# Attention stage of a fused kernel: output product from split parts, turns and products between the queries, key-value products in pairs

## What is computed

```python
B, L, D = x.shape
H, dh = (HEADS, HEAD_DIM)          # 16 heads of 16
q = relu(x @ Wq) / SCALE; k = relu(x @ Wk) / SCALE
v = x @ Wv;  u = silu(x @ Wu)      # each split into heads
kv = jnp.einsum('bhlk,bhlv->bhkv', k, v)
out = jnp.einsum('bhlk,bhkv->bhlv', q, kv)
out = srms_norm(out) * u           # by the root of the mean square of a head's 16 values
return out.transpose(0, 2, 1, 3).reshape(B, L, D) @ Wo
```

## Time and profile before

| what | value |
|---|---|
| median of 3 runs | 1888.03 us (1887.62 to 1890.15) |
| profiled execution, its own time | 1887.28 us |
| its span | 1885.6 us |
| PE busy | 1742.8 us (92%) |
| attention stage, first to last record | 1310.5 to 1486.6 us |
| loop bodies 1, 2, 3 | 41.32, 41.17, 41.17 us |
| last batch, up to the next stage's first matmul | 32.13 us |
| granted clock of the whole span | 0.974 of 2.4 GHz |

### The profile page before, as it was taken

One profiled execution on the slowest core, in us unless ns is written; L12 is line 12 of the kernel. 1 busy time (PEld: TensorE's weight loads), 2 busy tenths in 40 slices (PEclk: granted clock), 3 DMA queues, 4 the chain that ended last, 5 costly groups with the idle time before them and its releaser, 6 DMA issues. The chain is left out here.

```text
span 1885.6 us, 26501 instructions
## 1 busy us (share of the span) xinstructions
PE 1742.8 (92%) x9613; PEld 1381.1 (73%) x9613; DVE 1432.4 (76%) x2198; ACT 1079.3 (57%) x1866; POOL 1060.5 (56%) x633
## 2 busy tenths in 40 slices
PE   6888989899898989877899999999999899999999
PEld 2456666666556566655788888888888688888888
DVE  4899999999999999999777566666355755655665
ACT  6777787877777786787433433334444443334433
POOL 3889999999999999999722101112445411110111
PEclk9898999999999999988999999999999999999999
DMA  6223233233333233253000000000000000000000
GB/s 197 84 80 107 95 105 97 87 111 96 97 97 105 95 104 101 91 170 98 1 1 1 1 1 1 1 23 6 1 0 0 1 12 12 12 12 12 12 11 12
DMA packets 59109, 101.40 MB, mean 54 GB/s; under 512 B 11120, under 2 KB 11248, under 8 KB 58864
## 3 DMA queue, kind: packets, MB, share of 16 engines
q1 hardware_dynamic: 58992, 99.88, 16.6%
HBM read 95.14 MB, written 4.72 MB: 53 GB/s over the span
## 5 line engine op out<-in xcount | busy, mean ns | idle before, releaser
L383 POOL TENSOR_TENSOR m_U<-m_U,m_C 128x1024 f32<-128x1024 f32 x255 | 600.8, 2369 | 25.7 <-DVE m_U L890 15.5
L525 PEld LDWEIGHTS m_y<-ident,m_U 128*128 128x128 f32 x2048 | 252.6, 148 | 118.0 <-issue 70.9
L890 DVE TENSOR_TENSOR_SCAN m_U<-m_dA,m_carry,m_U 128x512 f32<-128x512 f32 x256 | 310.6, 1263 | 5.1 <-ACT m_dA L758 4.8
L525 PE MATMUL m_y<-ident,m_U 128*128 128x128 f32 x2048 | 284.8, 285 | 30.3 <-POOL m_U L383 30.2
L890 DVE TENSOR_TENSOR_SCAN m_U<-m_dA,m_U 128x512 f32<-128x512 f32 x256 | 295.9, 1203 | 11.5 <-ACT m_dA L758 8.2
L758 ACT ACTIVATE m_dA<-high,m_negA 128x512 f32<-128x512 f32 x256 | 172.3, 685 | 71.5 <-DVE m_U L890 71.1
L758 ACT ACTIVATE m_dA<-even,m_negA 128x512 f32<-128x512 f32 x256 | 170.7, 684 | 54.0 <-DVE m_U L890 53.0
L1123 POOL TENSOR_TENSOR SW<-g_Rt 128x1024 f32<-128x1024 f32 x16 | 31.6, 1996 | 252.6 <-ACT g_Rt L1308 252.6
L1123 POOL TENSOR_TENSOR SW<-f_Rt 128x1024 f32<-128x1024 f32 x16 | 31.6, 1995 | 205.2 <-ACT f_Rt L1308 205.2
L1303 ACT ACTIVATE g_sil<-g_psG 128x512 f32<-128x512 f32 x96 | 57.4, 598 | 140.2 <-PE g_psG L1181 139.6
L1303 ACT ACTIVATE f_sil<-f_psG 128x512 f32<-128x512 f32 x96 | 57.4, 598 | 134.9 <-PE f_psG L1181 134.2
(11 more groups left out here) (375 smaller groups left out, 4316.0 us busy)
## 6 DMA issues: line engine op xcount, KB each, us to landing
m_C<-bc_rows SPq DMA_DIRECT2D x256, 256.0 KB, 3.2
m_B<-bc_rows SPq DMA_DIRECT2D x60, 256.0 KB, 3.5
even<-in_ffn_w SPq DMA_DIRECT2D x16, 256.0 KB, 5.0
out<-res SPq DMA_DIRECT2D x8, 512.0 KB, 2.8
res<-in_x SPq DMA_DIRECT2D x1, 3072.0 KB, 13.0
res<-in_x SPq DMA_DIRECT2D x2, 512.0 KB, 4.3
turned<-in_Wkvqu SPq DMA_DIRECT2D x1, 1024.0 KB, 4.7
high<-in_in_w SPq DMA_DIRECT2D x1, 512.0 KB, 4.3
```

Source lines behind the costliest of these rows:

```text
L383: pool.tensor_tensor(u, u, C[:, M % C_RING, :].unsqueeze(1).to_broadcast([P, PE_E, CHUNK]), ALU.mult).then_inc(hc_ready, 1)
L525: last = nc.tensor.matmul(y[:, t, j * P:(j + 1) * P], U[:, M % U_RING, j, t * P:(t + 1) * P], ident[:, :], start=False, stop=n == N - 1, i ...
L890: nc.vector.tensor_tensor_scan(u, dA[:, s % A_RING, :], u, carry[:, e, n:n + 1] if q else 0.0, ALU.mult, ALU.add).then_inc(scan_done, 1)
```

## The change

The output product gets split operands: `wo` is split once into `wos`, and each turned pair of tiles into `ogs`, its high part by ScalarE's copy (`back`), its low part by a new VectorE step `low_og`. Turns no longer take a place in the ring's count (`JOBS` 16 to 12) but have semaphores of their own (`og_turned`, `og_high`, `og_low`). TensorE's order in a body changes, VectorE's `scale` of half 1 moves ahead of `keep_kv`, and key-value sums are taken two tiles at a time. The wait on `square_ready` goes.

```diff
+        wos = sb("wos", [P, 2, KD, D], FP32R)
...
-        ogT = sb("ogT", [P, TILES, D])
+        ogs = sb("ogs", [P, 2, TILES, D], FP32R)
...
-        KV, BACK, Q, JOBS = 0, (8, 14), 10, 16
+        WO_LANDED, WO_HIGH, WO_LOW = 16, 17, 18
+        KV, Q, JOBS = 0, 8, 12
...
@@ TensorE, keys_values @@
-                    if j > 0:
+                    if j % 2 == 0 and j > 0:
+                        heads_kv(n, first, j - 2)
                         heads_kv(n, first, j - 1)
+                heads_kv(n, first, SEQ_TILES - 2)
                 if behind is not None:
                     behind()
                 heads_kv(n, first, SEQ_TILES - 1)
...
-            def output(b, half, first):
+            def output(b, half):
                 for i in range(2):
-                    pe.wait_ge(ring_free, first + i + 1)
+                    pe.wait_ge(og_low, 2 * HALVES * b + 2 * half + i + 1)
                     pe.wait_ge(out_free, 2 * HALVES * b + 2 * half + i + 1)
                     for h in range(2):
-                        for g in range(KD):
-                            last = nc.tensor.matmul(acc[:, i, h * D:(h + 1) * D],
-                                                    ogT[:, 2 * i + h, g * P:(g + 1) * P], wo[:, g, :],
-                                                    start=g == 0, stop=g == KD - 1)
+                        last = split_mm(acc[:, i, h * D:(h + 1) * D],
+                                        [([x[:, 2 * i + h, g * P:(g + 1) * P] for x in og_parts],
+                                          [m[:, g, :] for m in wo_parts]) for g in range(KD)])
                     last.then_inc(out_full, 1)
...
@@ TensorE, the body @@
-                output_turn(b, 0, 1, start(b) + BACK[0])
+                output_turn(b, 0, 1)
+                first = start(b) + Q
+                pe.wait_ge(og_low, 2 * HALVES * b + 1)
+                query(first, 0)
                 pe.wait_ge(kvh_ready, b + 2)
-                output(b, 0, start(b) + BACK[0])
-                queries(start(b) + Q)
+                output(b, 0)
+                query(first, 1)
+                pe.wait_ge(ring_free, first + 1)
+                output_turn(b, 1, 0)
+                pe.wait_ge(ring_free, first + 2)
+                output_turn(b, 1, 1)
                 for i in range(2):
-                    output_turn(b, 1, i, start(b) + BACK[1])
-                output(b, 1, start(b) + BACK[1])
+                    pe.wait_ge(og_low, 2 * HALVES * b + 2 + i + 1)
+                    query(first, 2 + i)
+                output(b, 1)
...
@@ ScalarE @@
+            def back(b, half, i):
+                act.wait_ge(og_turned, 2 * HALVES * b + 2 * half + i + 1)
+                nc.scalar.activation(ogs[:, 0, 2 * i:2 * i + 2, :].rearrange("p h d -> p (h d)"), ring[:, i, :],
+                                     ACT.Copy).then_inc(og_high, 1)
...
@@ VectorE @@
+            def low_og(b, half, i):
+
+                dve.wait_ge(og_high, 2 * HALVES * b + 2 * half + i + 1)
+                high, low = (ogs[:, part, 2 * i:2 * i + 2, :].rearrange("p h d -> p (h d)") for part in range(2))
+                nc.vector.tensor_tensor(low, ring[:, i, :], high.bitcast(FP32), ALU.subtract).then_inc(og_low, 1)
...
                 scale(b, 0)
+                scale(b, 1)
+                low_og(b, 0, 0)
                 keep_kv(b + 1)
-                scale(b, 1)
+                low_og(b, 0, 1)
...
@@ VectorE, last_sequence @@
+                for i in range(2):
+                    low_og(b, 0, i)
                 late = slice(TILES, SEQ_TILES)
...
                 add_output(b, 0)
+                for i in range(2):
+                    low_og(b, 1, i)
                 add_output(b, 1, True)
...
```

More of the change, by code:

```diff
@@ L1633, in _ @@
         def _(pe):
+            og_parts = [ogs[:, part, :, :] for part in range(2)]
+            wo_parts = [wos[:, part, :, :] for part in range(2)]
             def split_mm(out, terms):
@@ L1703, in heads_out, with output_turn @@
                     last.then_inc(ou_full, 1)
-            def output_turn(b, half, i, first):
-                pe.wait_ge(ring_free, first + i - 1)
+            def output_turn(b, half, i):
                 for h in range(2):
@@ L1743, in _ @@
             keys_values(0, KV)
-            queries(FIRST_Q)
-            pe.wait_ge(w_o, 16)
+            for i in range(KD * HALVES):
+                pe.wait_ge(ring_free, FIRST_Q + i - 1)
+                query(FIRST_Q, i)
+            pe.wait_ge(w_o, WO_LOW)
             with pe.Fori(0, BATCH - 1) as b:
@@ L1788, in keys_values, with query @@
                     nc.scalar.activation(kv[:, j, D:], ring[:, j % 2, D:], ACT.Copy).then_inc(ring_free, 1)
-            def queries(first):
-                for half in range(HALVES):
-                    for g in range(KD):
-                        i = KD * half + g
-                        act.wait_ge(ring_full, first + i + 1)
-                        nc.scalar.activation(qT[:, g, half * CHUNK:(half + 1) * CHUNK], ring[:, i % 2, :], ACT.Relu,
-                                             scale=Q_SCALE).then_inc(ring_free, 1)
+            def query(first, i):
+                half, g = divmod(i, KD)
+                act.wait_ge(ring_full, first + i + 1)
+                nc.scalar.activation(qT[:, g, half * CHUNK:(half + 1) * CHUNK], ring[:, g, :], ACT.Relu,
+                                     scale=Q_SCALE).then_inc(ring_free, 1)
             def heads_out(b, half):
@@ L1816, in _ @@
                 keys_values(start(b) + KV)
-                back(start(b) + BACK[0])
-                queries(start(b) + Q)
-                back(start(b) + BACK[1])
+                for half in range(HALVES):
+                    for i in range(2):
+                        back(b, half, i)
+                    for i in range(2):
+                        query(start(b) + Q, KD * half + i)
             for half in range(HALVES):
@@ L1835, in _ @@
                                      ACT.Copy)
-            back(start(BATCH - 1) + 2)
+            for i in range(2):
+                back(BATCH - 1, 1, i)
         @block.vector
@@ L1974, in _ @@
             nc.vector.tensor_scalar(norms.var[:, EARLY], norms.mv[:, EARLY, 1], EPS, None, ALU.add).then_inc(var_ready, 1)
+            for i in range(2):
+                low_og(BATCH - 2, 1, i)
             add_output(BATCH - 2, 1)
```

52 lines of the change are left out of this document (25 added, 27 removed).

## The result

The changed kernel takes 1901.41 us (median of 6 runs, 1900.58 to 1903.77) against 1888.42 us for the kernel before (6 runs, 1887.62 to 1890.15) in the same comparison. The ratio is 1.007, with a 95% interval of 1.0057 to 1.0083: slower, by more than the 0.2% that can be told from none. The profiled execution took 1901.13 us with a span of 1899.4, 13.85 more than the one before.

What follows compares the result with a forecast made beforehand. TensorE's order of work was taken as the bound in the attention bodies. Terms -5.2 + 8.5 + 4.0 + 2.5 = +9.8 us, with clock falls of +4.5 and +0.5 making +14.8, gave 1902.8 us; range 1896.5 to 1909.0.

Steps and rivals of the forecast that it cites:

- the case given as likeliest: Attention stage: both stalls come, with falls of TensorE's clock as reckoned; 1902.8 us, chance 0.55.
- First stall: After a body's first turns, TensorE waits for low_og behind VectorE's late scale of half 1; +8.5 us over three bodies.
- Second stall: After a body's second turns, TensorE waits for low_og behind add_output and statistics; +1.3 us per body, +4.0 in sum.
- the third body's link: Second stall in the third body: VectorE has one link more there, adding 0.1 us.
- Last batch: Before the last product, the second pair of low_og stands behind add_output with its statistics; +2.5 us.
- Split product: Output product on TensorE: 24 split matmuls replace 16 fp32 ones, saving 0.65 us per half over 8 halves; -5.2 us.
- Pairs: Key-value products taken in pairs free no waiting TensorE work; 0, with bounds of -0.5 and +0.5 us.
- Prologue: Splitting wo once, 0.6 us on ScalarE and 0.7 on VectorE, is hidden while TensorE runs queries; 0.
- The clock: TensorE's clock falls at the first stall, 1.5 us per body, +4.5; +0.5 for the last batch's longer pause.
- Rival (a): Attention stage: the stalls come but TensorE's clock stays up; +9.8 us, 1897.8 us, chance 0.22.
- Rival (c): Second half's factors are no brake, no first stall or clock fall; +1.3 us, 1881 without other waits; chance 0.05.
- (d): No difference: stalls and savings cancel within 0.2%, 3.8 us; chance 0.06.

Runs made afterwards that it cites:

- e5: Kernel before with only VectorE's scale of half 1 moved ahead of keep_kv, output product still fp32; 1898.92 us, ratio 1.0057.
- e1: Changed kernel with VectorE's scale of half 1 put back behind keep_kv and both low_og of half 0; 1891.53 us, ratio 1.0017.
- e10: Changed kernel with GpSimd's power for half 1 of each body taken over 8 of 16 heads; 1892.06 us, ratio 1.0022.
- e4: Changed kernel with twelve unread 512-column matmuls on TensorE in each body's first stall; 1898.99 us, ratio 1.0059.
- e2: Changed kernel with low_og of half 1 ahead of the tokens' statistics, in bodies and last batch; 1900.17 us, ratio 1.0066.
- e11: e7 with the output product in plain fp32 and no low_og; 1886.49 us, ratio 0.9995.
- e7: Changed kernel with body turns in ou's banks, two queries ahead of each product, VectorE's scale and statistics behind low_og; 1881.45 us, ratio 0.9963.
- e6: Kernel before with the key-value sums in pairs alone; 1888.16 us, ratio 1.0000.
- e8: Split output product and paired key-value sums, with TensorE's order of the kernel before; 1886.78 us, ratio 0.9993.
- e9: Changed kernel with six unread 512-column matmuls in each body's first stall; 1899.36 us, ratio 1.0061.
- e3: Changed kernel with the edits of e1 and e2 together; 1885.29 us, ratio 0.9987.

## Why the prediction was right

1902.8 us was predicted, 1901.41 measured, and the case given as likeliest is the one that came. The rise was over-forecast a little more than the total shows: +14.8 was predicted; the medians rose by 13.0 and the profiled executions by 13.85. The kernel before came out 0.4 higher in this comparison than in the one that the prediction had. Step by step:

- **Where the stall comes from.** "Nobody on TensorE's path needs the second half's factors yet" was the fact, and the new order made someone need them. Shown from three sides: e5 makes the stall with that exchange alone, e1 takes it away by undoing it, e10 takes it away by shortening the power.
- **First stall, +8.5.** The distance from second turn to next work grew by 2.64, 2.85 and 2.55: +8.0. e4 against e1 gives 7.8.
- **Second stall, +4.0.** First turn to next query grew by 1.2, 1.2 and 1.0: +3.4. The extra 0.1 for the third body's link did not show. The statistics are the wait that ends last, as predicted, but e2 shows that with them out of the way only 0.55 of the 1.2 us goes.
- **Last batch, +2.5.** 3.60 for 1.29: +2.3.
- **Split product, -5.2.** 24 records last 3.04 us, the last of them 0.28, so they follow each other by 2.76 / 23 = 0.120, where the 49 records of the next stage gave 0.1167. 24 take 2.88, and 0.57 per half is saved: -4.6. The term was mis-sized in the change's favour, by 0.6 us, and e11 against e7 has the same 0.57. The four passes of true fp32 of which the Trainium skill tells ("FP8 and Floating Point Precision", TensorE Precision Notes) would have made it 0.86 by the prediction's estimate: the trace does not agree.
- **Pairs, 0.** e6: 0.1 us.
- **Prologue, 0.** From the stage's first matmul to body 1 it takes 20.96 us, before 20.97.
- **The clock, +4.5 and +0.5.** The size was right, the places were not. The prediction had three falls in the bodies at 1.5 each; two came, at 1.56 and 1.26 by e4, and none in the third body, though it was idle for 2.87 us. That the third did not come is luck of the execution as far as the runs show: e2, with the same pause, had it. So the body that stayed at 43.6 us lies outside the 44 to 46 that the prediction named. In the last batch a fall was added that had a price of its own: 2.46 - 2.3 + 1.14 = 1.3 us is what remains for it, 1.5 by e2, where 0.5 was put. Together 1.56 + 1.26 + 1.3 = 4.1 against 5.0. The Trainium skill ("TensorE: Matmul & The Clock Gate", HAM oscillation) has the throttle come back with every long pause of a loop: bodies 1 and 2 of the trace agree, body 3 does not.

At full clock the measured parts are 8.0 + 3.4 + 2.3 - 4.6 = +9.1 where +9.8 was predicted. With 4.1 for the clock and 0.26 for the later start it makes 13.5 of the 13.85; of the rest, 0.4, some 0.24 stands in body 1 and was not followed.

Rival (a), stalls without falls in the bodies, is what e4 made: 1897.8 was given, 1898.99 measured. Rival (c) is e10: +1.3 us was given for it, and e1 and e10 lie 3.6 and 4.5 above the kernel before, in the main because the last batch keeps its added fall and the split saves less. Its two figures also do not agree: `scaled` over by 1400 is 2.24 us before 1402.24, and the power was to be 2.9 shorter. The 1881 us that (c) gave for all waits gone is what e7 reached, 1881.45. (d) did not come in the changed kernel.

## What to carry to other kernels

Before moving work ahead of a wait, look for the latest input of the step that is moved past, even if nobody waits for it yet: here a factor that came 28 us into each body, at no cost, stopped TensorE as soon as its reader stood one place earlier on VectorE. Compare the saving with the length of the path that the new operand adds (turn, copy, subtraction), and put independent matmuls there first: the same split product was worth nothing in the bodies of e8 and 1.14 us in each of e7. And count a stall of TensorE at its length and the clock's fall that may come with it, here 1.3 to 1.6 us each, behind idle stretches of 1.75 to 3.3 us, though not behind all of them. One profiled execution does not tell whether a fall belongs to a kernel.

## What the runs showed that was not expected

- The length of the last idle stretch does not decide whether the clock falls. The first stall of body 3 left TensorE idle for 2.87 us in the changed kernel, without a fall, and for 2.88 in e2, with one; 1.75 us brought a fall in e9's body 2. In the last batch a pause of 2.36 to 2.43 us stands in all thirteen kernels; ten profiled executions have a fall with it, and e3, e9 and e11 have none. Body 1 of the changed kernel with a fall, its body 3 without, and body 3 of e2 with one (TensorE's timelines):

```profile
1361.81 2.36 PE L1644 MATMUL a_ring<-z_att,ws 128*128 128x512 f32 x6 [2.95 <-DVE a_ogs L1916]
```

```profile
1452.55 1.66 PE L1644 MATMUL a_ring<-z_att,ws 128*128 128x512 f32 x6 [2.87 <-DVE a_ogs L1916]
```

```profile
1452.42 2.93 PE L1644 MATMUL a_ring<-z_att,ws 128*128 128x512 f32 x6 [2.88 <-DVE a_ogs L1916]
```

  Six matmuls took 2.36, 1.66 and 2.93 us. The Trainium skill ("TensorE: Matmul & The Clock Gate", Part 1: The HAM clock gate) calls the stretch over which activity is judged free-running, so that a pause can meet it in another phase; that would fit, and no run here was made to test it.
- Matmuls that compute nothing made two bodies shorter, by 1.56 and 1.26 us, when they filled a stall (e4).
- GpSimd's power goes by elements, in the two sizes seen: 10.55 us for a 128x64 tile and 5.43 for 128x32 (e10).
- fp32 matmuls set in among split ones cost nothing for the change of type that e6 could tell: seven groups or four per batch made 0.1 us, with an interval of 0.9991 to 1.0009.
